# Decoder layer on one core: the cross-attention output turned and divided on VectorE in 32 x 32 blocks

## The chip, the cores and the metric

One core of a Trainium2 chip runs the whole kernel. The metric is device time in microseconds; the kernel before takes 612.61 us, the median of three runs between 610.9 and 614.4.

## What is computed

The input is x, 16 batches of 256 tokens with 256 features in float32. Three sublayers follow each other, each with a residual and a layer norm behind it (post-norm): a linear attention with relu features, a cross attention to a context of 256 tokens, and a low-rank feed-forward. The change touches the end of the cross attention:

```python
q = (query @ Wq.T), k = (key @ Wk.T), v = (value @ Wv.T)   # 16 heads of 16 features
q, k = rope2d(fp16(q), qpos), rope2d(fp16(k), kpos)
attn = softmax(q @ k^T * 16 ** -0.5)
x = (attn @ v).transpose(0, 2, 1, 3).reshape(B, Nq, C)
return x @ Wo.T + bo
...
x = layernorm(x + xattn(x, ctx, ...))
x = layernorm(x + gelu(x @ U1 @ V1 + b1) @ U2 @ V2 + b2)
```

## The kernel before

Every engine has its instruction list written out by hand, and semaphores tie them together. The main loop is unrolled over steps b = -3 to 15, and in a step several batches are in flight: batch b has its softmax and weighted sums computed, b + 1 its row maxima (`scores1`, `row_max`), b + 2 its q projection, b + 3 its linear attention; p = b - 1 is the batch whose attention output is divided, turned and projected, and q = b - 2 the one that goes through the second norm and the first feed-forward product. A step has eight slots. Each slot starts on TensorE with `scores1(b + 1, slot)`, which waits until VectorE's `row_max` of the slot before has emptied the one buffer SA, and `scores2(b, ...)`, which waits until ScalarE's exponential has emptied SB. The rest of each slot on every engine is listed in `step` of that engine, in strict order. So one engine that is late in a slot holds the others at the next score product.

The attention output of a batch goes this way. `pv` (line 1219) writes the weighted sums feature-major into the two PSUM banks BK[0] (first half of the heads) and BK[1]: 32 partitions for a head, of which 16 are features, the 17th the sum of the weights (the ones in `v_aug`), and 4 groups of heads by 256 tokens. ScalarE copies each bank to SBUF in `ev_pv` (line 633), to `o_fm`. TensorE turns it to token-major in `o_t` (line 1236), eight 128 x 128 transposes into BK[1] and FR[1]. VectorE takes the reciprocals (line 939) and multiplies (line 942) into `lin_tm` in `att_norm`. TensorE turns the result back in `att_t` (line 1133, BK[1]), four transposes. ScalarE copies it twice in `ev_att`: the high half, rounded to the matrix format (line 655), and the value itself (line 656, `att_raw`). GpSimd subtracts for the low half in `att_lo` (line 479). TensorE multiplies high and low halves with Wo in `wo` (line 1051, BK), and VectorE adds the residual in `add2` (line 950), takes statistics (line 887), and GpSimd normalises (`norm2`, lines 500 and 504) and keeps a copy with a bias (`keep_x2`, line 511).

Other pieces of the order that matter below: on TensorE `p_ff` (line 1264) follows `wo`, and `v2`, the v projection, goes into BK[0] and so waits until the first half of the weighted sums has left it. On VectorE a step runs `add1`, `ev_shift`, `row_max` 0, `stats2(q)`, `row_max` 1, `stats1`, `row_max` 2, `att_norm`, `row_max` 3, `k_halves`, `ev_x1`, `vk`, `row_max` 4, `rope_q` (lines 842, 859, 861), `ev_p` (line 907), `row_max` 5, `add2`, `lin` (lines 828 to 834), `row_max` 6, `rope_q_sum`, `lint`, `row_max` 7, `shift`. On GpSimd it runs `norm2(q)`, `rstd1`, `split_x` (lines 441 and 443), `att_lo`, `rope_k` (lines 467, 469, 473), `keep_x2(q)`, `residual2` (line 494), `residual_bias` (line 456), `split_c` (lines 441 and 443). SyncE places the turned k by eight DMAs once `rope_k` is done. After the last step the first block of the feed-forward (lines 1370, 1380, gelu at line 750) is interleaved by hand with what is left of batches 14 and 15; a loop over seven more blocks follows.

Of the kernel before, what the change touches and what calls it, by code (L numbers as in the profile page):

```python
# [31 lines left out]
P = 128  # L32
# [40 lines left out]
def build(nc, a):  # L73
    ctx = ExitStack()
    with ctx:
# [9 lines left out]
        def parts(name, shape):  # L85
# [78 lines left out]
        o_fm = sb("o_fm", [P, H2 // HC, T])  # L164

        stage_v1 = o_fm[:].rearrange("p q t -> p (q t)")


        rden2 = sb("rden2", [P, TT, H2])
# [62 lines left out]
        s_ot_mm, s_att_mm, s_wo_mm, s_x2t_mm, s_p_mm = map(  # L232
            sem, ("s_ot_mm", "s_att_mm", "s_wo_mm", "s_x2t_mm", "s_p_mm"))
# [347 lines left out]
        def _(act):  # L581
# [48 lines left out]
            def ev_pv(b, half):  # L630

                act.wait_ge(s_pv_mm, NQ * b + NQ // 2 * (half + 1))
                act.activation(o_fm[:, 2 * half:2 * half + 2].rearrange("p q t -> p (q t)"), BK[half][:], ACT.Copy
                               ).then_inc((s_pvc_ev, s_pvd_ev)[half], 1)

# [46 lines left out]
            def step(b):  # L682
# [12 lines left out]
                if on(p):  # L695
                    ev_pv(p, 1)
# [26 lines left out]
                if on(b):  # L723
                    exp_chunk(b, 4)
                    ev_pv(b, 0)
# [19 lines left out]
            ev_pv(LAST, 1)  # L745
# [34 lines left out]
        def _(dve):  # L780
# [177 lines left out]
            def step(b):  # L958
# [13 lines left out]
                if on(n):  # L972
                    stats1(n)
# [22 lines left out]
                if on(n1):  # L996
                    row_max(n1, 5)
# [486 lines left out]
```

## Time and profile before

| | us |
|---|---|
| median of three runs | 612.61 (610.9 to 614.4) |
| the profiled execution, its own time | 611.63 |
| its span on the core | 609.8 |
| TensorE busy | 531.0 (87%) |
| VectorE busy | 401.0 (66%) |
| ScalarE busy | 344.7 (57%) |
| GpSimd busy | 281.4 (46%) |
| the chain that ended last | TensorE 57%, VectorE 15%, issue 14%, GpSimd 6%, ScalarE 5% |

Busy time is a sum over the whole span; the chain is the sequence of work that the end waited for, followed back from the last instruction. What counts below is the row of steps between 100 and 440 us, which all look the same, and the end of the steps between 440 and 525 us.

### The profile page before, as it was taken

How to read it: one execution, taken by the hardware profiler on the slowest of the kernel's cores; microseconds unless marked ns; L12 is line 12 of the kernel's file. 1: busy time of each engine (PE TensorE's matmuls, PEld its weight loads, DVE VectorE, ACT ScalarE, POOL GpSimd, SP SyncE). 2: the span in 40 equal slices, each digit the busy share in tenths (PEclk: the TensorE clock that was granted, in tenths of full speed). 3: DMA queues.
4: the chain of work that ended last, by engine and by line, in shares of the span. 5: the costliest groups of instructions: out<-in, count | busy, mean ns of one | idle time of the engine just before them, and what ended most of it. 6: DMA issues, size and time to landing. Idle time of an engine off the chain costs nothing.

```text
span 609.8 us, 11786 instructions
## 1 busy us (share of the span) xinstructions
PE 531.0 (87%) x4224; PEld 366.8 (60%) x4224; DVE 401.0 (66%) x906; ACT 344.7 (57%) x503; POOL 281.4 (46%) x321
## 2 busy tenths in 40 slices
PE   0763879999999999999999999999987777999993
PEld 0652656767676767767676767677654444555551
DVE  4431688786968787777869687877877532253534
ACT  4420236756665666657566656666565566546551
POOL 3608526255564556364554645562624222233324
PEclk9995999999999999999999999999979889999997
DMA  7750120120202020111202020201101002032322
GB/s 263 177 140 14 53 65 13 55 63 5 83 2 82 7 77 27 57 34 51 79 5 84 2 82 7 79 26 41 29 3 31 19 1 70 17 104 103 104 102 103
DMA packets 27209, 35.99 MB, mean 59 GB/s; under 512 B 5592, under 2 KB 13400, under 8 KB 27160
## 3 DMA queue, kind: packets, MB, share of 16 engines
q1 hardware_dynamic: 26440, 34.90, 18.4%
q8 instruction: 32, 0.52, 0.4%
q10 hardware_dynamic: 720, 0.43, 0.3%
q14 instruction: 17, 0.14, 0.1%
HBM read 23.51 MB, written 8.65 MB: 53 GB/s over the span
## 4 chain that ended last, share of the span: by engine, by line
PE 57%; DVE 15%; issue 14%; POOL 6%; ACT 5%; DMA 2%; SPq 1%; POOLq 0%; ACTq 0%
PE FR L1051 20%; PE BK L1219 7%; PE BK L1051 7%; DVE nmax L914 6%; PE SC L1177 5%; PE SC L1204 3%; PE FR L1133 3%; PE FR L1109 2%; PE FR L1264 2%; DVE lin_tm L834 2%; POOL rs L568 2%; PE BK L1236 2%; POOL c_fm L573 2%; DVE y L950 1%; DVE rden L830 1%
## 5 line engine op out<-in xcount | busy, mean ns | idle before, releaser
L914 DVE TENSOR_REDUCE nmax<-SC 128x4 f32<-128x1024 f32 x128 | 156.2, 1220 | 42.1 <-PE SC L1177 41.1
L680 ACT ACTIVATE probs<-SC 128x1024 f32<-128x1024 f32 x128 | 131.1, 1024 | 69.9 <-PE SC L1204 69.6
L1177 PE MATMUL SC<-k_blk,q_grp 48*128 48x512 f16 x256 | 51.0, 395 | 27.1 <-DVE nmax L914 18.0
L1219 PE MATMUL BK<-probs,v_aug 128*32 128x256 f32 x1024 | 69.9, 390 | 0.5 <-ACT probs L680 0.5
L479 POOL TENSOR_TENSOR att_fm_l<-att_raw,att_fm_h 128x512 fp32r<-128x512 f32 x16 | 20.5, 1283 | 76.5 <-ACT att_raw L656 76.5
L500 POOL TENSOR_TENSOR rs<-ve,minus_half 128x2 f32<-128x2 f32 x16 | 11.2, 701 | 94.6 <-DVE nm L956 94.6
L1204 PE MATMUL SC<-q_grp,k_blk 64*128 64x256 f16 x512 | 50.3, 275 | 3.4 <-ACT q_grp L638 1.6
L750 ACT ACTIVATE probs<-SC,b_ff 128x512 f32<-128x512 f32 x64 | 39.8, 687 | 22.5 <-PE SC L1370 21.7
L1177 PEld LDWEIGHTS SC<-k_blk,q_grp 48*128 48x128 f16 x256 | 12.4, 93 | 54.8 <-issue 22.6
L1051 PE MATMUL FR<-w_qkv_h,xs_fm_h 128*128 128x512 f32 x64 | 29.2, 456 | 16.6 <-POOL xs_fm_l L443 14.1
L1219 PEld LDWEIGHTS BK<-probs,v_aug 128*32 128x32 f32 x1024 | 26.8, 110 | 25.9 <-issue 14.2
L609 ACT ACTIVATE kv_tm<-FR 128x512 f32<-128x512 f32 x32 | 19.1, 598 | 35.4 <-PE FR L1051 35.1
L1204 PEld LDWEIGHTS SC<-q_grp,k_blk 64*128 64x128 f16 x512 | 25.0, 97 | 21.2 <-ACT probs L680 4.1
L1380 PE MATMUL FR<-probs,w_u 128*64 128x512 f32 x128 | 35.5, 614 | 0.3 <-DVE xs_fm_l L1027 0.2
L568 POOL TENSOR_TENSOR rs<-ve,minus_half 128x2 f32<-128x2 f32 x16 | 11.0, 689 | 46.9 <-DVE nm L1039 46.9
L494 POOL TENSOR_TENSOR x1b<-x_tm,b_o 128x512 f32<-128x512 f32 x16 | 20.8, 1300 | 22.9 <-DVE y L950 22.9
L486 POOL TENSOR_TENSOR rs<-ve,minus_half 128x2 f32<-128x2 f32 x16 | 11.2, 698 | 42.9 <-DVE nm L896 42.9
L1034 DVE TENSOR_TENSOR x_fm<-BK,x_tm 128x512 f32<-128x512 f32 x16 | 10.4, 687 | 28.0 <-PE BK L1391 27.9
L1051 PEld LDWEIGHTS FR<-w_qkv_h,xs_fm_h 128*128 128x128 f32 x64 | 12.5, 196 | 26.1 <-POOL xs_fm_l L443 14.0
L1370 PE MATMUL SC<-p_fm,w_v_h 128*128 (+1 forms) x64 | 28.0, 438 | 0.0
L1051 PE MATMUL FR<-w_qkv_h,xs_fm_l 128*128 128x512 f32 x64 | 26.2, 409 | 0.0
L1051 PE MATMUL FR<-w_qkv_l,xs_fm_h 128*128 128x512 f32 x64 | 26.2, 409 | 0.0
(170 smaller groups left out, 1542.8 us busy)
## 6 DMA issues: line engine op xcount, KB each, us to landing
x_fm<-in_x_fm SPq DMA_DIRECT2D x16, 256.0 KB, 3.0
c_fm<-in_c_fm SPq DMA_DIRECT2D x16, 256.0 KB, 3.6
x_tm<-in_x_tm SPq DMA_DIRECT2D x16, 256.0 KB, 2.9
x_kept<-x2b SPq DMA_DIRECT2D x16, 256.0 KB, 2.3
x_tm<-x_kept SPq DMA_DIRECT2D x16, 256.0 KB, 2.8
out<-c_fm SPq DMA_DIRECT2D x16, 256.0 KB, 2.0
k_blk<-k_rope SPq DMA_DIRECT2D x128, 16.0 KB, 1.8
q_grp<-q_grp SPq DMA_DIRECT2D x32, 32.0 KB, 1.9
```

The costliest lines, as they stand in the source:

```text
L479: pool.tensor_tensor(flat(att_fm[1][:]), flat(att_raw[:]), flat(att_fm[0][:]).bitcast(F32), ALU.subtract).then_inc(s_attt_ev, 1)
L494: pool.tensor_tensor(x1b[:, n % NB], x1_tm[:], b_o2[:].unsqueeze(1).broadcast_to([P, TT, C]), ALU.add).then_inc(s_x1b, 1)
L568: pool.tensor_tensor(rs3[:, h], ve3[:, h], minus_half[:], ALU.pow).then_inc(s_rs3, 1)
L680: act.activation(probs[:, j % 4], SB[:], ACT.Exp, scale=SCALE).then_inc(s_exp, 1)
L750: act.activation(gel[:, f % 4], SC[f % 4 // 2][:].rearrange("p h t -> p (h t)")[:, FB * (f % 2):FB * (f % 2) + FB], ACT.Gelu_apprx_tanh, b ...
L914: dve.tensor_reduce(nmax[:, t, :, 2 * q:2 * q + 2], SA[:].rearrange("p (s f) t -> p s f t", s=2), AX.X, ALU.max, negate=True).then_inc(s_m ...
L1051: mm = pe.matmul(out, lhs(i, c), rhs(j, c), start=(c + k == 0), stop=(c + k == CC + 1))
L1177: mm = pe.matmul(SA[:, 2 * s:2 * s + 2].rearrange("p h t -> p (h t)"), q_grp[n % NB][rows, q, t * P:(t + 1) * P], k_blk[n % NB][rows, q].r ...
L1204: mm = pe.matmul(SB[:, 2 * s + f], k_blk[b % NB][rows, q, f, t * P:(t + 1) * P], q_grp[b % NB][rows, q], start=True, stop=True)
L1219: mm = pe.matmul(BK[q // 2][HP * k:HP * (k + 1), (q % 2) * T:(q % 2 + 1) * T], v_aug[b % NB][:, t, HC * q + k], probs[:, j % 4, k], start= ...
L1370: mm = pe.matmul(out, w_v1[k][:, f * P:(f + 1) * P], p_fm[:, bass.ds(i * FB, FB)], start=(k == 0), stop=(k == 1))
L1380: pe.matmul(FR[0][R * k:R * k + R, :], w_u2[:, f + k], gel[:, (f + k) % 4], start=(f == 0), stop=(f == NF - 2)).then_inc(s_u2_mm, 1)
```

## The change

The twelve TensorE transposes of a step and ScalarE's copies of the weighted sums go. VectorE turns each bank of weighted sums straight from PSUM in 32 x 32 blocks (`turn_pv`) into `o_tok`, where a partition holds a token of a block and a free index the head's features and weight sum. It takes one reciprocal, multiplies in two instructions into `lin_tm`, and turns that again in 32 x 32 blocks into `att_raw` in SBUF. The features come out in another order, which the rows of Wo are given on the host. ScalarE makes the high half from `att_raw` alone. The calls move as shown: `turn_pv(p, 1)` stands behind `stats1` and ahead of `row_max` 2, `turn_pv(b, 0)` behind `row_max` 5, and `add2` ahead of `row_max` 5. After the last step the orders of VectorE, ScalarE and TensorE change too.

```diff
-            def ev_pv(b, half):
-                act.wait_ge(s_pv_mm, NQ * b + NQ // 2 * (half + 1))
-                act.activation(o_fm[:, 2 * half:2 * half + 2].rearrange("p q t -> p (q t)"), BK[half][:], ACT.Copy
-                               ).then_inc((s_pvc_ev, s_pvd_ev)[half], 1)
             def ev_att(p):
-                act.wait_ge(s_att_mm, p + 1)
-                act.activation(flat(att_fm[0][:]), BK[1][:], ACT.Copy).then_inc(s_att_hi, 1)
-                act.activation(flat(att_raw[:]), BK[1][:], ACT.Copy).then_inc(s_att_raw, 1)
+                act.wait_ge(s_att_raw, p + 1)
+                wait(act, s_wo_mm, p)
+                act.activation(flat(att_fm[0][:]), flat(att_raw[:]), ACT.Copy).then_inc(s_att_hi, 1)
...
+            act.wait_ge(s_pv_mm, NQ * B)
             gelu(0, 0)
             gelu(0, 1)
             ev_att(LAST)
-            gelu(0, 2)
-            gelu(0, 3)
+            for f in range(2, 6):
+                gelu(0, f)
             ev_x2t(LAST - 1)
-            gelu(0, 4)
+            gelu(0, 6)
             ev_p(LAST - 1)
-            for f in range(5, NF):
-                gelu(0, f)
+            gelu(0, 7)
...
+            def turn_pv(b, half):
+                dve.wait_ge(s_pv_mm, NQ * b + NQ // 2 * (half + 1))
+                dve.transpose(o_tok[:, 2 * half:2 * half + 2].rearrange("p q b r -> p (q b r)"), BK[half][:]
+                              ).then_inc((s_pvc_ev, s_pvd_ev)[half], 1)
             def att_norm(p):
-                o = [t[:].rearrange("p (h r) -> p h r", r=HP) for t in (FR[1], BK[1])]
-                for k, t in enumerate((1, 0)):
-                    dve.wait_ge(s_ot_mm, 2 * p + k + 1)
-                    dve.reciprocal(rden2[:, t], o[t][:, :, D2]).then_inc(s_rden2, 1)
-                for k, t in enumerate((1, 0)):
-                    dve.wait_ge(s_rden2, 2 * p + k + 1)
-                    dve.tensor_tensor(lin_tm[:, t].rearrange("p (h d) -> p h d", h=H2), o[t][:, :, 0:D2],
-                                      rden2[:, t].unsqueeze(2).broadcast_to([P, H2, D2]), ALU.mult
+                dve.wait_ge(s_pvc_ev, p + 1)
+                dve.wait_ge(s_pvd_ev, p + 1)
+                dve.reciprocal(rden2[:], o_tok[:, :, :, D2]).then_inc(s_rden2, 1)
+                dve.wait_ge(s_rden2, p + 1)
+                out = flat(lin_tm[:]).rearrange("p (q b u d) -> p q b u d", q=2, b=T // HP, u=2)
+                for half in range(2):
+                    part = slice(2 * half, 2 * half + 2)
+                    dve.tensor_tensor(out[:, :, :, half], o_tok[:, part, :, 0:D2],
+                                      rden2[:, part].unsqueeze(3).broadcast_to([P, 2, T // HP, D2]), ALU.mult
                                       ).then_inc(s_att_ev, 1)
+                dve.wait_ge(s_att_ev, 2 * p + 2)
+                wait(dve, s_attt_ev, p)
+                dve.transpose(flat(att_raw[:]), flat(lin_tm[:])).then_inc(s_att_raw, 1)
...
                 if on(n):
                     stats1(n)
+                if on(p):
+                    turn_pv(p, 1)
...
-                if on(n1):
-                    row_max(n1, 5)
                 if on(p):
                     add2(p)
+                if on(n1):
+                    row_max(n1, 5)
+                if on(b):
+                    turn_pv(b, 0)
                 if on(m):
                     lin(m)
...
+            turn_pv(LAST, 1)
+            att_norm(LAST)
             stats2(LAST - 1)
-            att_norm(LAST)
             add2(LAST)
...
-            def vk(m, p):
+            def vk(m):
                 pe.wait_ge(s_kv1_ev, 2 * m + 2)
-                if on(p):
-                    pe.wait_ge(s_att_ev, 2 * p + 2)
...
-                if on(p):
-                    o_t(p, 1)
-                    o_t(p, 0)
...
-                if on(p):
-                    att_t(p)
                 if on(m):
-                    vk(m, p)
+                    vk(m)
...
-            o_t(LAST, 1)
-            o_t(LAST, 0)
...
             h_ff(0, 0)
             h_ff(0, 1)
-            att_t(LAST)
             h_ff(0, 2)
             h_ff(0, 3)
             u2_ff(0, 0)
             h_ff(0, 4)
             h_ff(0, 5)
+            wo(LAST)
+            u2_ff(0, 2)
             x2_t(LAST - 1)
-            wo(LAST)
             p_ff(LAST - 1)
-            u2_ff(0, 2)
             h_ff(0, 6)
             h_ff(0, 7)
```

## Rows read from the trace of the kernel before

**Rows 1.** Busy time by stretch: stretch, its length, each engine's busy us, clock, DMA share, GB/s.
```profile
core 0: us, PE busy (x) PEld busy (x) DVE busy (x) ACT busy (x) POOL busy (x), PEclk, DMA share, GB/s
298.85:326.79 27.94, 27.13 (x244) 19.64 (x244) 22.37 (x49) 18.02 (x27) 15.12 (x17) 1.00 0.15 46
438.52:511.14 72.62, 55.69 (x516) 32.60 (x516) 42.02 (x88) 42.66 (x57) 23.48 (x27) 0.88 0.08 26
511.14:525.79 14.65, 13.30 (x65) 7.74 (x65) 3.50 (x12) 9.05 (x15) 3.08 (x4) 1.00 0.05 19
```

**Rows 2.** The chain of waits of one step: start us, us, what (x instructions).
```profile
309.68 0.59 PE BK L1236 x4
...
310.26 0.44 PE FR L1236 x4
...
314.24 0.44 PE BK L1133 x4
...
315.66 0.32 PE SC L1177 x2
...
319.77 0.88 PE FR L1264 x4
...
321.94 1.23 DVE nmax L914
...
323.20 0.69 DVE y L950
...
326.79 0.39 PE SC L1177 x2
```

**Rows 3.** VectorE's timeline, same step: start us, us, instruction, idle before and its releaser.
```profile
309.50 1.23 DVE L914 TENSOR_REDUCE nmax<-SC 128x4 f32<-128x1024 f32 x1 [0.66 <-PE SC L1177]
...
311.27 0.41 DVE L942 TENSOR_TENSOR lin_tm<-FR,rden 128x256 f32<-128x256 f32 x1
...
312.47 1.22 DVE L914 TENSOR_REDUCE nmax<-SC 128x4 f32<-128x1024 f32 x1 [0.79 <-PE SC L1177]
...
319.34 0.45 DVE L859 TENSOR_TENSOR q_cos<-q,cos_t 128x512 f16<-128x512 f16 x1
...
319.72 1.37 DVE L861 TENSOR_TENSOR q_sin<-rot,sin_t 128x512 f16<-128x512 f16 x1
```

**Rows 4.** GpSimd's timeline, same step.
```profile
310.56 1.30 POOL L443 TENSOR_TENSOR xs_fm_l<-x_fm,xs_fm_h 128x512 fp32r<-128x512 f32 x1
...
315.99 1.28 POOL L479 TENSOR_TENSOR att_fm_l<-att_raw,att_fm_h 128x512 fp32r<-128x512 f32 x1 [4.13 <-ACT att_raw L656]
...
319.66 1.15 POOL L473 TENSOR_TENSOR k_rope<-k_cos,k_sin 128x512 f16<-128x512 f16 x1
```

**Rows 5.** Single source lines: ns min/median/max, first and last start us, form.
```profile
L950 DVE TENSOR_TENSOR y<-BK,x1b x16: 676/692/692, 127.7 to 520.3; 128x512 f32<-128x512 f32 x16
...
L808 DVE TENSOR_TENSOR w_v_l<-probs,w_v_h x1: 1422/1422/1422, 15.1 to 15.1; 128x512 fp32r<-128x512 f32 x1
...
L808 DVE TENSOR_TENSOR w_k_l<-x2b,w_k_h x1: 679/679/679, 16.4 to 16.4; 128x512 fp32r<-128x512 f32 x1
...
L842 DVE STREAM_SHUFFLE k_rot<-k x16: 436/439/442, 24.1 to 454.1; 128x256 uint32<-128x256 uint32 x16
...
L861 DVE TENSOR_TENSOR q_sin<-rot,sin_t x16: 412/1372/1479, 43.9 to 459.2; 128x512 f16<-128x512 f16 x16
```

**Rows 6.** The chain of waits of the last step.
```profile
494.29 0.61 ACT o_fm L633
...
500.26 1.27 POOL att_fm_l L479
```

**Rows 7.** Timeline across the end of the last step, VectorE and GpSimd.
```profile
506.17 0.75 DVE L887 BATCH_NORM_STATS2 st<-y 128x6 f32<-128x256 f32 x2
...
507.60 0.70 POOL L500 TENSOR_TENSOR rs<-ve,minus_half 128x2 f32<-128x2 f32 x1 [4.83 <-DVE nm L956]
...
509.58 1.27 POOL L511 TENSOR_TENSOR x2b<-x_tm,b_ff 128x512 f32<-128x512 f32 x1
...
517.19 1.29 POOL L479 TENSOR_TENSOR att_fm_l<-att_raw,att_fm_h 128x512 fp32r<-128x512 f32 x1 [6.34 <-ACT att_raw L656]
```

More of the change, by code:

```diff
@@ L163, in build @@
         shift16 = sb("shift16", [P, TT, P], F16)
-        o_fm = sb("o_fm", [P, H2 // HC, T])
-        stage_v1 = o_fm[:].rearrange("p q t -> p (q t)")
-        rden2 = sb("rden2", [P, TT, H2])
+        o_tok = sb("o_tok", [P, H2 // HC, T // HP, HP])
+        stage_v1 = o_tok[:].rearrange("p q b r -> p (q b r)")
+        rden2 = sb("rden2", [P, H2 // HC, T // HP])
         att_fm = parts("att_fm", [P, CC, T])
@@ L231, in build @@
         s_s1_mm, s_shift_mm, s_s2_mm, s_pv_mm = map(sem, ("s_s1_mm", "s_shift_mm", "s_s2_mm", "s_pv_mm"))
-        s_ot_mm, s_att_mm, s_wo_mm, s_x2t_mm, s_p_mm = map(
-            sem, ("s_ot_mm", "s_att_mm", "s_wo_mm", "s_x2t_mm", "s_p_mm"))
+        s_wo_mm, s_x2t_mm, s_p_mm = map(sem, ("s_wo_mm", "s_x2t_mm", "s_p_mm"))
         s_h_mm, s_u2_mm, s_ff_mm = map(sem, ("s_h_mm", "s_u2_mm", "s_ff_mm"))
@@ L694, in step @@
                     exp_chunk(b, 0)
-                if on(p):
-                    ev_pv(p, 1)
                 if on(m):
@@ L724, in step @@
                     exp_chunk(b, 4)
-                    ev_pv(b, 0)
                 if on(b):
@@ L744, in _ @@
             exp_chunk(LAST, 7)
-            ev_pv(LAST, 1)
             act.sem_inc(s_gelu, 4)
@@ L994, in step @@
                     ev_p(q)
+                if on(p):
+                    add2(p)
                 if on(n1):
                     row_max(n1, 5)
-                if on(p):
-                    add2(p)
+                if on(b):
+                    turn_pv(b, 0)
                 if on(m):
@@ L1222, in pv @@
                 mm.then_inc(s_pv_mm, 1)
-            def o_t(p, t):
-                if t == 1:
-                    pe.wait_ge(s_pvc_ev, p + 1)
-                    pe.wait_ge(s_pvd_ev, p + 1)
-                elif on(p + 4):
-                    pe.wait_ge(s_kv1_ev, 2 * (p + 4) + 1)
-                elif p + 4 == B:
-                    pe.wait_ge(s_proj_ev, B)
-                else:
-                    pe.wait_ge(s_p_ev, p - 1)
-                for q in range(H2 // HC):
-                    mm = pe.transpose((FR[1], BK[1])[t][:, q * P:(q + 1) * P], o_fm[:, q, t * P:(t + 1) * P], ident[:])
-                mm.then_inc(s_ot_mm, 1)
-            def att_t(p):
-                pe.wait_ge(s_att_ev, 2 * p + 2)
-                turn(BK[1], lin_tm, s_att_mm)
             def wo(p):
@@ L1255, in x2_t @@
                     pe.wait_ge(s_vk_ev, q + 6)
-                if q == LAST:
-                    pe.wait_ge(s_p_ev, LAST)
+                elif q + 5 == B:
+                    pe.wait_ge(s_proj_ev, B)
+                else:
+                    pe.wait_ge(s_p_ev, q)
                 turn(FR[1], x2_tm, s_x2t_mm)
@@ L1293, in step @@
                     scores2(b, 1)
-                if on(p):
-                    o_t(p, 1)
-                    o_t(p, 0)
                 if on(kn):
@@ L1307, in step @@
                     x1_t(n, m, kn)
-                if on(p):
-                    att_t(p)
                 if on(m):
-                    vk(m, p)
+                    vk(m)
                 if on(n1):
@@ L1446 @@
     by_group = [D2 * h + d for h in HEADS for d in range(D2)]
+    by_turned = [D2 * HEADS[HC * (2 * half + q) + k] + d
+                 for q in range(2) for k in range(HC) for half in range(2) for d in range(D2)]
     inv_freq = np.float32(1.0) / np.float32(100.0) ** (np.arange(0, 8, 2, dtype=np.float32) / np.float32(8))
@@ L1457 @@
         "w_v2": chunks(get["L0_xattn_Wv"].T[:, by_group]).reshape(P, -1),
-        "w_o2": chunks(get["L0_xattn_Wo"].T[by_group]).reshape(P, -1),
+        "w_o2": chunks(get["L0_xattn_Wo"].T[by_turned]).reshape(P, -1),
         "w_u1": chunks(get["L0_ffn_U1"]),
```

## The prediction

> **What bounds the kernel now.** I read the busy time by stretch first. One batch step, from the last score product of a batch to that of the next, takes 27.94 us, and TensorE is busy for 27.13 us of it at full granted clock; VectorE is busy for 22.37, ScalarE 18.02, GpSimd 15.12 [rows 1]. Steps 1 to 12 are alike, so twelve steps are the body of the kernel, the last three steps take 72.62 us at a mean clock of 0.88, and the start of the feed-forward part, up to the last batch's x2 transpose, takes 14.65 us [rows 1]. TensorE looks like the only bound, but the chain of waits says otherwise. From 309.68 to 320.65 it runs through TensorE without a gap: the attention output's transposes (0.59 and 0.44), the transposes of the divided output (0.44), the projections, and `p_ff` at its end [rows 2]. From there to the next score product at 326.79 it runs through VectorE: `row_max` 5 at 321.94, `add2` at 323.20, the linear attention's division, `row_max` 6 [rows 2]. A step is therefore some 21.8 us of TensorE order and 6.1 us of VectorE order. The third view is VectorE's timeline: it idles 0.66 us ahead of `row_max` 2 and 0.79 ahead of `row_max` 3 [rows 3]. That is all the room that lies beside the TensorE part at this place.
>
> **What the change does to a step.** It removes twelve TensorE transposes: 0.59 + 0.44 + 0.44 = 1.47 us of the chain [rows 2]. It removes three ScalarE copies out of PSUM; the fourth, for the high half, now reads SBUF. ScalarE is not on the chain here, so I cost these at nothing; what covers them is its 9.9 us of idle time per step, and no cover is lost. It adds three block transposes of 128 x 512 words to VectorE and turns the two reciprocals of 16 into one of 32.
>
> The price of a turn is in no row. The nearest by size and source is the 512-word read of PSUM in `add2`, 0.692; the nearest by kind is the shuffle of 256 words, 0.439; a turn that took each word twice would cost what `row_max` costs for 1024 words, 1.23 [rows 2, 5]. The bounds are 0.44 and 1.23. I take 0.70, because read and written words are the same as in `add2`, and the shuffle shows that moving words between partitions adds nothing that is seen.
>
> The Trainium skill (VectorE: DVE Perf Modes, The three transpose paths) gives 311 ns for a 128 x 128 bf16 transpose on VectorE, made of 32 x 32 blocks. With one more element per cycle at its 0.96 GHz this makes 0.71 us for 512, an estimate; it says nothing of four-byte words.
>
> Turn of the second half (`turn_pv(p, 1)`): it stands ahead of `row_max` 2, where VectorE idles 0.66 [rows 3]. 0.70 fits but for some 0.05. Free.
>
> The division (`att_norm`): it now starts right after `row_max` 2, at 310.80, and no longer waits for TensorE. Its products read both inputs from SBUF. GpSimd runs the subtraction for the next batch from 310.56 to 311.86 [rows 4], and two-input products of that sort are seen to wait for GpSimd: the product that began at 319.72 with GpSimd's own at 319.66 lasted 1.37 us where the shortest of its 16 took 0.412, and at the start of the kernel one weight half took 1.422 where its equals take 0.679 [rows 3 to 5]. So: reciprocal 0.3 to 311.15, first product held to 311.86 and done 0.3 later, second 0.35, 312.5. The third turn brings it to 313.2, `row_max` 3 (1.23) to 314.4. TensorE, 1.47 earlier, wants the fourth score product at 315.66 - 1.47 = 314.19 [rows 2]. It waits 0.2. With the small costs of that wait the front part gains 1.25 us.
>
> This hold is the Trainium skill's (SBUF — State Buffer, Who interferes with whom): a VectorE instruction with two SBUF inputs contends with a GpSimd one that reads SBUF, and the later one blocks until the first has finished. It speaks against this change, whose products read PSUM before; the 1.422 beside 0.679 agrees.
>
> Turn of the first half (`turn_pv(b, 0)`): it stands between `row_max` 5 and `lin`, inside the stretch where VectorE is the chain. Nothing hides it: +0.70. `add2` only trades places with `row_max` 5, both inside the stretch; the fifth score product starts 0.7 later after its own row maximum, where TensorE has `lin` and then idles. `v2` now waits for this turn instead of ScalarE's copy; it has 1.45 us to run and is through before `lin`'s division ends, so `lin_t` behind it waits for VectorE as it does today. ScalarE's `ev_att` waits for the third turn; it is ready about 313.2, when ScalarE is with the x1 copy. GpSimd's low half then begins at some 314.6 in place of 315.99 [rows 4], and `wo`, wanted at about 317.1, doesn't wait. No DMA is moved; the placement of k follows the low half on GpSimd and comes earlier.
>
> Net per step: -1.25 + 0.70 and 0.05 of seams = -0.5 us. Twelve steps: -6.0. Step 0 has the first-half turn with nothing removed: +0.7.
>
> **The last three steps.** Transposes run at half the clock there, and the route itself is on the chain: in the last step from ScalarE's copy at 494.29 to the end of the low half at 501.53, 7.24 us [rows 6]. The new route is 0.7 turn, 1.1 division, 0.7 turn, 0.7 copy, 1.3 low half and 0.5 for the exponential that ScalarE has in front: 5.0, so -2.2. The step before gives 1.6 by the same sum and pays 0.8 back at `add2` and the first-half turn. In step 13 the low half stands ahead of the k rotation whose placement ends the wait for the last scores: -2.2. Together -5.0, an estimate good to 2.
>
> **The start of the feed-forward part.** Here an order changes that costs. VectorE takes `turn_pv`, `att_norm`, and only then the statistics of batch 14, which today are done at 506.17, under the exponentials [rows 7]. GpSimd's order is unchanged: normalise batch 14, add the bias (from 507.60 to 510.85), and only then the low half of batch 15, at 517.19 [rows 7]. From the end of the last weighted sums: turn and division 2.7, statistics 1.4, GpSimd 3.3, low half 1.3: `wo` starts at 8.8 where it starts at 7.4 today. Behind it come, in TensorE's new order, a down-projection (1.0), the x2 transpose of 14, `p_ff`, and ScalarE's `ev_p` now behind the seventh gelu; VectorE's statistics of batch 15 wait for that. My sum to the last x2 transpose is 19.7 against 14.65 [rows 1]: +5.0, again good to 2. TensorE stands behind it in order, so it is all on the path; the loop after it is not touched.
>
> **Sum.** -6.0 + 0.7 - 5.0 + 5.0 = -5.3 us on the profiled execution's 611.63, so 606.3. That execution lies 1.0 under the median of the three runs, well inside their spread; I keep its own time as the base. About 0.5%, 3 us, is what a measurement of this kernel can tell from no change.
>
> **Rivals.**
> 1. *GpSimd's hold reaches the rotation of q.* Today the sine product ends at 321.09, 0.4 ahead of its need [rows 3]. `p_ff` comes 1.25 earlier, GpSimd's rotation of k 1.4 earlier. Its last product then starts at 318.2, and VectorE's cosine product, at 319.34 now, at 318.15: a dead heat. If GpSimd wins, the cosine product is held by the rotation and the sine product by the bias addition after it, and `row_max` 5 starts 0.7 late. The step is +0.2: 611.6 + 2.4 + 0.7 = 614.7. For it: the 1.37 us median; against it: the gap between GpSimd's two products. Chance 0.22.
> 2. *A turn costs 1.23.* The slower end. Place: the first-half turn in VectorE's stretch (+0.53), the other two in front of `row_max` 2 and 3 (+0.7 after idle time and hold are used up). A step is +0.7: +8.4, +0.7 and some 1.2 at the end: 622. It decides from a turn of about 0.92 us, where the step's gain is gone. Against it: the shuffle's price. Chance 0.14.
> 3. *The hold does not bite in the division.* Then `row_max` 3 ends in time and the step gives 0.75: 603.3. Chance 0.12.
> 4. *TensorE's clock.* Its idle time between the fifth and sixth score products grows from 0.7 to about 2 us. In the last steps, where it waited longer, the mean clock is 0.88 [rows 1]. If the granted clock fell to 1.2 GHz once per step, some 1.4 us of products would take twice as long: over 620. In all twelve steps today it is 1.00. Chance 0.05.
> 5. *It doesn't do what it says:* the removed transposes are made good by another wait, the exponentials or `row_max`, and the step stays 27.94: about 612. Chance 0.04.
>
> The forecast keeps 0.43; its own range is 602 to 610, from the two ends' estimates.
>
> **The numbers.** The range is 600 to 619: it takes in rivals 1, 3 and 5 and part of 2, and leaves out about 0.2. Faster by over 0.5%: the forecast but for 0.05, and rival 3: 0.50. Within: that 0.05, rival 5, and 0.14 of rival 1: 0.23. Slower: rivals 2 and 4 and the rest of 1: 0.27.
>
> **What would show it.** A turn at 0.70 us; the step at 27.4; `row_max` 3 later by 0.5 or more than `row_max` 2's end plus 2.0, with the first product longer than the second; the sine product ending before `ev_p` can start; the wait ahead of the last score product of a batch grown to over 1 us; the low half of batch 15 later than today against the last weighted sums. A turn over 0.9, or a product in the rotation that lasts beyond GpSimd's bias addition, makes the forecast wrong.

## The result: slower, 629.59 us, and the profile after

The kernel after takes 629.59 us, the median of four runs between 627.16 and 633.02. The kernel before, on the same chip, takes 613.13. The ratio is 1.0276, with an interval of 1.0217 to 1.0336. The forecast was 606.3, and its range ended at 619.

The profiled execution took 633.02 us, with a span of 631.2 against 609.8. TensorE is busy for 523.5 us (before 531.0), VectorE for 452.3 (401.0), ScalarE for 320.3 (344.7), GpSimd for 280.8 (281.4). From the page of the kernel after, part 4, the shares of the chain that ended last:

```profile
PE 36%; DVE 33%; issue 20%; POOL 5%; ACT 3%; DMA 1%; POOLq 0%; SPq 0%; DVEq 0%
```

Before, TensorE had 57% of that chain and VectorE 15%. The work did leave TensorE, but the path went with it. The windows of the kernel after, cut as in [rows 1] (one step, the last three steps, the start of the feed-forward part, and then the loop):

```profile
core 0: us, PE busy (x) PEld busy (x) DVE busy (x) ACT busy (x) POOL busy (x), PEclk, DMA share, GB/s
308.12:336.99 28.87, 26.14 (x230) 18.41 (x232) 26.18 (x51) 16.48 (x24) 15.05 (x17) 1.00 0.14 45
451.63:524.09 72.46, 55.38 (x481) 29.62 (x482) 47.13 (x88) 38.24 (x48) 19.64 (x22) 0.79 0.08 25
524.09:546.38 22.29, 15.50 (x53) 8.10 (x53) 6.05 (x19) 8.10 (x13) 6.06 (x8) 0.85 0.03 12
546.38:631.20 84.82, 73.94 (x328) 41.88 (x328) 34.89 (x121) 40.81 (x67) 29.44 (x49) 0.96 0.27 96
```

A step went from 27.94 to 28.87, though TensorE is busy for 0.99 us less in it. VectorE went from 22.37 to 26.18. That is 3.81 more where the three turns are 2.12, so some 1.7 us of it is VectorE's other instructions taking longer and not VectorE doing more. The spans differ by 21.4 us (the profiled execution is 3.4 over its median), and it adds up like this: 4.3 up to the first full step, 8.8 in twelve steps, -0.2 in the last three steps, 7.6 at the start of the feed-forward part, 0.8 in the loop. Of the twelve steps nine are longer by 0.9, one by 0.4, the last by 0.2, and the first, 26.88 us in both kernels, by nothing.

VectorE's timeline of that step in the kernel after; its counterpart is [rows 3]:

```profile
318.49 0.71 DVE L926 STREAM_TRANSPOSE o_tok<-BK 128x512 f32<-128x512 f32 x1
...
320.38 0.34 DVE L933 RECIPROCAL rden<-o_tok 128x32 f32<-128x32 f32 x1
320.76 1.45 DVE L938 TENSOR_TENSOR lin_tm<-o_tok,rden 128x256 f32<-128x256 f32 x2
322.25 0.71 DVE L943 STREAM_TRANSPOSE att_raw<-lin_tm 128x512 f32<-128x512 f32 x1
...
328.56 1.21 DVE L848 TENSOR_TENSOR q_cos<-q,cos_t 128x512 f16<-128x512 f16 x1
329.70 1.49 DVE L850 TENSOR_TENSOR q_sin<-rot,sin_t 128x512 f16<-128x512 f16 x1
331.22 0.43 DVE L896 TENSOR_TENSOR p_fm<-FR,p_hi 64x256 fp32r<-64x256 f32 x1
...
333.42 0.70 DVE L926 STREAM_TRANSPOSE o_tok<-BK 128x512 f32<-128x512 f32 x1
...
336.85 1.45 DVE L856 TENSOR_TENSOR q_grp<-q_cos,q_sin 128x512 f16<-128x512 f16 x1
```

GpSimd's timeline of the same step, its counterpart is [rows 4]:

```profile
320.30 1.29 POOL L442 TENSOR_TENSOR xs_fm_l<-x_fm,xs_fm_h 128x512 fp32r<-128x512 f32 x1
...
328.34 1.16 POOL L472 TENSOR_TENSOR k_rope<-k_cos,k_sin 128x512 f16<-128x512 f16 x1
329.46 1.46 POOL L510 TENSOR_TENSOR x2b<-x_tm,b_ff 128x512 f32<-128x512 f32 x1
...
336.75 1.27 POOL L442 TENSOR_TENSOR cs_fm_l<-c_fm,cs_fm_h 128x512 fp32r<-128x512 f32 x1
```

Lay the two beside each other. The division's products (320.76) end at 322.21, 0.6 after GpSimd's subtraction (320.30 to 321.59). The cosine product (328.56) ends 0.27 after GpSimd's k_rope ends; the sine product begins 0.24 after GpSimd's bias addition and ends 0.27 after it. The sum of the two (336.85) begins 0.10 after another subtraction, ends 0.28 after it, and takes 1.45 us; the shortest of its 16 takes 0.402. In what follows, such a product is called held.

The whole trace of the kernel after has 54 VectorE products with two inputs in SBUF (a pair counted once) that start while a GpSimd instruction that reads SBUF runs; 53 of them end 0.27 us or more after it. The odd one, at 443.73, starts 0.02 us behind GpSimd's k_rope (443.71) and takes 0.41, and k_rope takes 1.43: at so small a distance the times don't tell who was first. In the kernel before, four products of 512 columns start under GpSimd's memsets, which read nothing, and take 0.68 each; their equal that starts under a subtraction takes 1.42 [rows 5].

The sum of the rotation was held before too, but for less, by the rounding that stands ahead of GpSimd's subtraction. VectorE and GpSimd in the kernel before:

```profile
326.64 0.78 DVE L867 TENSOR_TENSOR q_grp<-q_cos,q_sin 128x512 f16<-128x512 f16 x1
```
```profile
326.54 0.61 POOL L441 TENSOR_SCALAR cs_fm_h<-c_fm 128x512 fp32r<-128x512 f32 x1
```

Against the last score product S of a batch, GpSimd's rounding starts at S - 0.94 in the kernel after and its subtraction at S - 0.24, where it was S - 0.25 and S + 0.45 before; the sum starts at S - 0.14 in both. So it now meets the subtraction.

What the step's 0.93 us is made of, counted from S (298.85 before, 308.12 after; before in brackets): the first projection behind it starts at S + 1.98 (S + 1.61), because the sum of the rotation is held; TensorE is through with q at S + 19.45 (19.49); `ev_p` starts at S + 23.10 (22.64); the next S is at 28.87 (27.94). So +0.37, then -0.41 in the front part, then +0.50 through the rotation, and +0.47 in VectorE's stretch with the turn.

The chain of waits of the kernel after, from the division to the transposes of x2, shows why the front part gave so little (compare [rows 2], where the same place is TensorE without a gap):

```profile
320.76 0.04 DVE lin_tm L938
320.79 1.00 issue
321.80 0.42 DVE lin_tm L938
322.25 0.71 DVE att_raw L943
322.96 1.06 DVE nmax L903
324.01 0.42 DVE k_rot L831
324.44 0.57 DVE x_fm_l L890
325.01 0.37 DVE vk_sb L809
325.38 0.14 issue
325.52 0.63 PE FR L1135 x4
```

The "issue" of 1.00 inside the division is the hold. Behind the row maximum come the shuffle of k, the low half of x1 and the copy of v and k, and only then may TensorE go on with the transposes of x2, which stand ahead of q's projection in its order.

### The profile page after: what moved, and what is told of

Its sections match the earlier page's. It is cut to its first block, busy times and chain, and to the rows that moved or that the text cites. A ratio compares the mean times of both kernels' runs of the same rounds, so it can differ in the third digit from the quotient of the medians.

```text
span 631.2 us, 11408 instructions
## 1 busy us (share of the span) xinstructions
PE 523.5 (83%) x4032; PEld 351.5 (56%) x4032; DVE 452.3 (72%) x938; ACT 320.3 (51%) x455; POOL 280.8 (44%) x321
## 4 chain that ended last, share of the span: by engine, by line
PE 36%; DVE 33%; issue 20%; POOL 5%; ACT 3%; DMA 1%; POOLq 0%; SPq 0%; DVEq 0%
PE FR L1055 17%; DVE nmax L903 9%; PE BK L1055 6%; PE BK L1221 3%; PE SC L1179 3%; DVE q_grp L856 3%; PE FR L1135 2%; DVE q_sin L850 2%; DVE q_cos L848 2%; DVE lin_tm L823 2%; POOL rs L567 2%; POOL c_fm L572 2%; DVE lin_fm_l L862 2%; DVE o_tok L926 2%; PE SC L1206 2%
## 5 line engine op out<-in xcount | busy, mean ns | idle before, releaser
L1221 PE MATMUL BK<-probs,v_aug 128*32 128x256 f32 x1024 | 72.8, 404 | 0.5 <-ACT probs L673 0.5
L1206 PE MATMUL SC<-q_grp,k_blk 64*128 64x256 f16 x512 | 51.9, 282 | 4.7 <-ACT probs L673 2.7
L1358 PE MATMUL FR<-probs,w_u 128*64 128x512 f32 x128 | 36.8, 629 | 0.7 <-ACT probs L739 0.7
L1135 PE MATMUL FR<-ident,x_tm 128*128 128x128 f32 x128 | 21.8, 295 | 10.9 <-DVE vk_sb L809 5.9
L1135 PEld LDWEIGHTS FR<-ident,x_tm 128*128 128x128 f32 x128 | 14.3, 147 | 23.8 <-issue 17.3
L926 DVE STREAM_TRANSPOSE o_tok<-BK 128x512 f32<-128x512 f32 x32 | 22.6, 706 | 6.7 <-PE BK L1221 6.7
```

The source lines that it names most:

```text
L926: dve.transpose(o_tok[:, 2 * half:2 * half + 2].rearrange("p q b r -> p (q b r)"), BK[half][:]).then_inc((s_pvc_ev, s_pvd_ev)[half], 1)
L1135: mm = pe.transpose(dst[:, c * T + t * P:c * T + (t + 1) * P], src[:, t, c * P:(c + 1) * P], ident[:])
L1206: mm = pe.matmul(SB[:, 2 * s + f], k_blk[b % NB][rows, q, f, t * P:(t + 1) * P], q_grp[b % NB][rows, q], start=True, stop=True)
L1221: mm = pe.matmul(BK[q // 2][HP * k:HP * (k + 1), (q % 2) * T:(q % 2 + 1) * T], v_aug[b % NB][:, t, HC * q + k], probs[:, j % 4, k], start= ...
L1358: pe.matmul(FR[0][R * k:R * k + R, :], w_u2[:, f + k], gel[:, (f + k) % 4], start=(f == 0), stop=(f == NF - 2)).then_inc(s_u2_mm, 1)
```

## Experiments

**1 and 2. GpSimd narrowed, in the kernel after and in the kernel before.** The same edit in both (shown for the subtractions). It leaves out most of GpSimd's subtractions for the inputs, its rotation of k and its kept copy of x2: they run over 32 of 512 columns, and the rest keeps old values.

```diff
-                pool.tensor_tensor(lo, x, hi.bitcast(F32), ALU.subtract).then_inc(s_lo, 1)
+                w = 2 * T if m < 2 else 32
+                pool.tensor_tensor(lo[:, 0:w], x[:, 0:w], hi.bitcast(F32)[:, 0:w], ALU.subtract).then_inc(s_lo, 1)
```

> The changed kernel, with GpSimd's two-input products narrowed: the low halves of x and the context from batch 2 on to 32 of 512 columns, the rotation of k from batch 1 on to 32 of 512, and the kept copy of x2 from batch 2 on to 32 of 512; the rest of these values is stale. All waits, orders and VectorE instructions stay. Theory 1 (GpSimd holds VectorE's products that read two SBUF inputs: the division, the rotation of q and the sum of the rotation): the products fall back to 0.42 us, a step from 28.87 to about 27.8 us, the kernel to about 616 us. Rival (the three turns alone fill VectorE, and the holds lie in idle time): at most 0.3 us per step, so 626 us or more.

> The kernel before with the same narrowing of GpSimd's products, as the control. Theory 1: there the holds lie beside other waits (the sine product ends 0.4 us before its need, the sum of the rotation ends before TensorE wants the projection), so a step loses at most 0.1 us: 610 to 613 us. If the holds were a cost of this kernel too, it would fall as much as the changed one, to about 600 us, and they would not explain the difference.

Measured: after, narrowed, 609.29 (ratio to before 0.9915, 0.9883 to 0.9947); before, narrowed, 608.06 (0.9918, 0.9887 to 0.9949). The narrowing takes 20.3 us from the kernel after and 5.9 from the kernel before. The two are then 1.2 us apart, within their intervals, though not alike inside: the step falls from 28.86 to 27.70 in the one and stays at 27.94 in the other, while the start of the feed-forward part still takes 20.3 us in the one and 14.7 in the other. The products are free: cosine 0.412, sine 0.418, sum 0.424, a division product 0.422.

```profile
L859 DVE TENSOR_TENSOR q_grp<-q_cos,q_sin x16: 404/424/439, 45.9 to 456.7; 128x512 f16<-128x512 f16 x16
```

So what made the step slow needs GpSimd's instructions at that length. A caution: the narrowing also hands over GpSimd's own results earlier; what that alone is worth was not taken apart. In the kernel before, and in version 6 (experiment 12), the same narrowing moved no step.

**3. VectorE's copy of v and k ahead of its low half of x1.**

```diff
-                if on(n):
-                    ev_x1(n)
                 if on(m):
                     vk(m)
+                if on(n):
+                    ev_x1(n)
```

> The changed kernel with VectorE's masked copy of the linear attention's sums (vk) ahead of its low half of x1, everything else as it is. Theory: what TensorE's removed transposes gain in the front of a step is lost at the x2 transpose, which waits for that copy, and VectorE reaches the copy late, behind row_max 3, the shuffle and the low half of x1; the copy earlier gives 0.3 to 0.4 us per step, about 625 us. Rival: the next score product or the q projection is as late as that, then nothing changes (628 to 631 us).

Measured: 620.11 (1.0106, 1.0065 to 1.0147), the step 28.02, so -0.84 instead of some -0.4. By the medians of eight steps, q's cosine product can start 0.31 earlier (S + 20.12 for 20.43), and that decides the race in the rotation the other way. The line of q's cosine product, kernel after and then this one (ns min/median/max of 16):

```profile
L848 DVE TENSOR_TENSOR q_cos<-q,cos_t x16: 409/1212/1286, 43.4 to 471.6; 128x512 f16<-128x512 f16 x16
```
```profile
L848 DVE TENSOR_TENSOR q_cos<-q,cos_t x16: 408/412/1004, 43.8 to 462.2; 128x512 f16<-128x512 f16 x16
```

It now starts ahead of GpSimd's k_rope and runs through in 0.41, and `ev_p` starts at S + 22.26 for 23.07: 0.31 us from the earlier q and 0.50 from the race. One move of 0.3 us is paid twice and more. The sum of the rotation is still held (median 1.447).

**4 and 5. The end.** In 4 only the statistics of batch 14 go back ahead of the turn; in 5 the orders of TensorE and ScalarE at the end also go back to those before.

```diff
+            stats2(LAST - 1)
             turn_pv(LAST, 1)
             att_norm(LAST)
-            stats2(LAST - 1)
```

> The changed kernel with VectorE's statistics of batch 14 ahead of the turn and division of batch 15 after the last step, as in the kernel before. Theory: GpSimd then normalises and keeps batch 14 under the last exponentials and the low half of batch 15 begins some 3 us earlier; the stretch from the last weighted sums to the last x2 transpose shrinks from 22.3 us to about 19, the kernel to about 626 us. Rival: the down-projection and the gelu order in front of it decide, and nothing changes.

> The changed kernel with the whole end as in the kernel before: statistics of batch 14 first on VectorE, x2 transpose of 14 ahead of wo and the down-projection on TensorE, gelu 4 ahead and gelu 5 to 7 behind ev_p(14) on ScalarE. Theory: the 7.6 us by which the stretch from the last weighted sums to the last x2 transpose grew are these orders; it falls from 22.3 to about 14 us, the kernel to about 621 us, some 4 us below the kernel with the statistics alone moved. Rival: TensorE's clock, at half in parts of that stretch (mean 0.85 against 1.00), keeps it at 18 us or more; then about 625.

Measured: 625.77 (1.0196, 1.0168 to 1.0224) and 622.59 (1.0127, 1.0079 to 1.0176). From the end of the last weighted sums to the last x2 transpose it is 22.3 us in the kernel after, 16.5 in 4, 13.2 in 5, and 14.65 before [rows 1]. The new orders at the end cost 7.0 us by the medians and 9.1 in this stretch, and with the old ones the turns make this stretch 1.4 us shorter than the transposes did.

Not all of the 9.1 is order. Experiment 3 keeps the orders of the kernel after here, and its stretch takes 19.8 us. In both, `wo` starts 8.6 us after the last weighted sums; behind it the clock differs. A part of the stretch in the kernel after, and the whole of it in experiment 3:

```profile
531.32:537.40 6.08, 4.76 (x16) 2.93 (x16) 0.69 (x1) 0.00 (x0) 1.26 (x2) 0.51 0.11 43
```
```profile
513.14:532.96 19.82, 13.02 (x52) 6.61 (x53) 6.05 (x19) 8.10 (x13) 6.06 (x8) 1.00 0.04 14
```

The profiled execution of the kernel after had half the clock for some 6 us, and that is 2.5 of its 22.3. Experiments 4 and 5 had 1.00 in the whole stretch, so at the same clock the two parts of the order cost 3.3 us each, 6.6 together, which agrees with the 7.0 of the medians.

**6. All three orders.** 3 and 5 together, and `lint`, the low half of the linear attention's output, for which TensorE's first projection waits, ahead of the sum of the rotation:

```diff
+                if on(m):
+                    lint(m)
                 if on(n):
                     rope_q_sum(n)
-                if on(m):
-                    lint(m)
```

> The changed kernel with the end of the kernel before, vk ahead of the low half of x1, and on VectorE the low half of the linear attention (lint) ahead of the sum of q's rotation. Theory: that sum is held by GpSimd's split of the context (1.44 us where 0.42 is free), and the projection on TensorE waits for lint behind it, 0.37 us per step; lint first frees it. A step of 27.65 us instead of 28.02, the kernel about 607 us (620.1 - 8 for the end - 4.5). Rival: the projection waits for something else, a step stays at 28.0, about 612.

Measured: 605.44 (604.27 to 606.74), ratio 0.9869 (0.9823 to 0.9914): 1.3% faster than the kernel before and 3.8% faster than the kernel after. Its windows, same cuts:

```profile
298.85:326.46 27.61, 26.20 (x231) 18.42 (x232) 24.55 (x50) 16.36 (x24) 15.25 (x17) 1.00 0.16 47
436.90:505.64 68.74, 50.74 (x481) 26.98 (x482) 47.15 (x94) 38.09 (x48) 22.57 (x26) 0.88 0.08 26
505.64:518.75 13.11, 11.67 (x52) 6.42 (x53) 4.92 (x13) 7.99 (x13) 3.23 (x5) 1.00 0.05 21
```

VectorE's timeline of the step. The division and the sine product are still held, the cosine product is not, and the sum (327.25) starts so late in GpSimd's subtraction that it is held for some 0.1 us only.

```profile
311.05 1.45 DVE L939 TENSOR_TENSOR lin_tm<-o_tok,rden 128x256 f32<-128x256 f32 x2
...
318.56 0.41 DVE L849 TENSOR_TENSOR q_cos<-q,cos_t 128x512 f16<-128x512 f16 x1
318.89 1.37 DVE L851 TENSOR_TENSOR q_sin<-rot,sin_t 128x512 f16<-128x512 f16 x1
320.68 0.43 DVE L897 TENSOR_TENSOR p_fm<-FR,p_hi 64x256 fp32r<-64x256 f32 x1 [0.42 <-ACT p_fm L663]
...
327.25 0.52 DVE L857 TENSOR_TENSOR q_grp<-q_cos,q_sin 128x512 f16<-128x512 f16 x1
```

`ev_p` starts at S + 21.83, 0.81 earlier than before, and the stretch behind it is 0.48 longer: the step gains 0.33. The last three steps give 3.9 us. The forecast had 0.5 and 5.0 for these two. The 3.9 is not a firm figure: the kernel after and experiments 4 and 5 have the same lists up to here, and their last three steps take 72.4, 70.0 and 71.7 us, so single executions differ by over 2 us in this place.

**7. The subtraction moved away from the division.** From 6, GpSimd's split for the next batch goes behind q's sine product, ahead of `keep_x2`:

```diff
-                if on(m + 1):
+                if b < -1 and on(m + 1):
                     split_x(m + 1)
...
+                if b >= -1 and on(m + 1):
+                    pool.wait_ge(s_q_part, 2 * n + 2)
+                    split_x(m + 1)
                 if on(q):
                     keep_x2(q)
```

> The same as three_orders, and GpSimd's split of the next x moved from ahead of the low half of the attention output to behind VectorE's sine product (with a wait for it), the kept copy of x2 behind that. Theory: the division's first product is no longer held (1.04 to 0.42 us), row_max 3 ends 0.6 us earlier, and the sine product is held at most once; a step of 27.3 to 27.5 us, about 604 us. Rival: TensorE's own order already sets the front part, so the step stays as in three_orders; or the moved split holds the rotation's sum later in the step and costs 0.2.

Measured: 609.06 (0.9914, 0.9887 to 0.9941), 3.6 us more than 6; the step is 27.87. The two division products now take 0.76 together and nothing comes of it: in the chain of waits, the way from ScalarE's copy of k and v to the transposes ahead of q's projection takes 6.18 us (311.50 to 317.68) as in 6 (309.18 to 315.36), and VectorE waits for TensorE there. GpSimd is late at the end of the step instead, and from its timeline and VectorE's:

```profile
301.15 1.29 POOL L442 TENSOR_TENSOR cs_fm_l<-c_fm,cs_fm_h 128x512 fp32r<-128x512 f32 x1
```
```profile
301.69 1.03 DVE L860 TENSOR_TENSOR q_grp<-q_cos,q_sin 128x512 f16<-128x512 f16 x1
```

The hold has moved to the sum of the rotation. `row_max` 7, the shift and `add1` stand behind the sum, and TensorE's first product with the next x starts at S + 4.38 for 4.10: this is the whole loss of the step. The division's hold, then, was real and is covered in 6.

**8. `add2` ahead of the sixth row maximum, in the kernel before.** The part of the change that has nothing to do with turns.

```diff
-                if on(n1):
-                    row_max(n1, 5)
                 if on(p):
                     add2(p)
+                if on(n1):
+                    row_max(n1, 5)
```

> The kernel before with only add2 moved ahead of row_max 5 on VectorE, as the change does. Theory: both lie in the same stretch of VectorE's order, nothing changes: 611 to 615 us, a step of 27.94. Rival: the fifth score product, 0.7 us later, delays the exponentials and v2 behind it and is part of the loss: 616 us or more.

Measured: 613.81 (0.9997, 0.9972 to 1.0022), which is no change of the time that could be told; the step in the trace is 27.80, 0.14 shorter. The order of [rows 2] shows where it comes from: `add2` behind the row maximum starts 1.26 us after it did (321.94 to 323.20), whereas the sum of the rotation starts 1.13 after one (307.99 behind 306.86 in the kernel after).

This run also tells what of the 4.3 us ahead of the first full step is not the change's. Its list up to there has no turn, and yet the first division of the linear attention starts at 105.23, against 101.72 before and 106.02 after. In the window from 62 to 90 us the mean clock is 0.86 here and 0.85 in the kernel after, where it was 0.97 before. With 3.5 of the 4.3 us also there without turns, 0.8 is left for the change, and that is no measurement: experiments 4 and 5, with the list of the kernel after up to there, reach the first full step 1.1 us later than it does.

**9. The orders without the turns.** The kernel before with two of the three orders, `vk` and `lint` as in 3 and 6 (the end has its old order anyway).

> The kernel before, with two of the three orders that the version at 605.4 us uses: VectorE's copy of v and k ahead of its copy of x1, and the division's transpose ahead of the sum of the two rotation products of q. No block turns. This asks whether that version's gain belongs to the turns or to the orders alone. Theory (the turns took a wait away from TensorE's order, and the new orders only undo the holds that the change brought): in the kernel before, TensorE's order sets the front part and q's cosine product is not held, so the step stays at 27.9 within 0.15 and the time within 0.5% of the kernel before (611 to 617). Rival (the orders are worth as much without the change): the step falls to 27.5 and the time to 608 or less, and the turns themselves are worth nothing or cost.

Measured: 619.94 (1.0094, 1.0066 to 1.0122), and the step is 28.56. Both expectations fall: the orders alone are neither neutral nor a gain, they cost 0.62 us per step. Most of it is a hold. With `lint` first, the sum of the rotation comes 0.9 us later than before and meets GpSimd's subtraction instead of the rounding ahead of it. VectorE's timeline and GpSimd's:

```profile
305.63 1.23 DVE L867 TENSOR_TENSOR q_grp<-q_cos,q_sin 128x512 f16<-128x512 f16 x1
```
```profile
305.29 1.29 POOL L443 TENSOR_TENSOR cs_fm_l<-c_fm,cs_fm_h 128x512 fp32r<-128x512 f32 x1
```

`row_max` 7, the shift and `add1` stand behind it in the chain of waits, and TensorE's first product with the next x starts at S + 4.57 for 4.10 before: 0.47 of the 0.62. In 6 GpSimd's subtraction starts at S - 0.25 instead of S + 0.46, so the sum, at S + 0.8 in both, takes 0.51 there. The rest shows at `vk`:

```profile
322.19 0.46 DVE L820 TENSOR_TENSOR vk_sb<-FR,vk_mask 128x288 f32<-128x288 f32 x1 [1.63 <-PE FR L1109]
322.56 0.68 DVE L901 TENSOR_TENSOR x_fm_l<-FR,x_fm_h 128x512 fp32r<-128x512 f32 x1
```

With `vk` first, VectorE waits 1.63 us for the v-k product, which stands behind the transposes of the divided output on TensorE, and the low half of x1, which q needs, comes behind that wait. That wait is long and costs little: q's projection takes 1.54 us in the chain where it took 1.41, so some 0.13. In 6, `vk` starts with no idle time ahead of it.

In the same orders the turns are worth 28.56 - 27.61 = 0.95 us per step, and 14.5 us in all. But half of that is the hold which `lint` first brings to the kernel without turns. Against the kernel before in its own order the turns with their orders are worth 0.33 per step. Whether `vk` first alone, or another order, would help the kernel without turns was not run.

**10. The third order alone.** 6 without the `lint` edit.

> The kernel after with the end in the order of before and VectorE's copy of v and k ahead of its copy of x1, but the sum of q's rotation left where it is. Against the version with all three orders it prices the third one alone. Theory: the sum of q's rotation is still held for 1.45 us, the division's transpose and the first projection start some 0.37 us late in each of thirteen steps, so the step is 28.0 and the time about 605.4 + 4.8 to 5.5 = 610 to 611. Rival (with the second order in place the sum of q's rotation is no longer on the path): the step is 27.65 and the time within 1.5 us of 605.4.

Measured: 610.28 (0.9951, 0.9925 to 0.9977), the step 28.01, the sum of the rotation 1.443. So with the low half behind it the hold costs 0.40 us per step, 4.8 us in twelve, and that is the whole difference to 605.44.

**11. One more turn per step.** In 6, the turn of the first half made twice, the second behind the first:

```diff
+                if half == 0:
+                    wait(dve, s_turn0, b)
+                    dve.transpose(out, BK[half][:]).then_inc(s_turn0, 1)
+                    dve.wait_ge(s_turn0, b + 1)
                 dve.transpose(out, BK[half][:]).then_inc((s_pvc_ev, s_pvd_ev)[half], 1)
```

> The version with all three orders, with the turn of the first half of the heads made twice, one behind the other, in each of sixteen steps: one more turn in VectorE's stretch between q's rotation and the last score product. Theory (that stretch is the path, nothing hides a turn there): 0.71 us and a seam of about 0.05 per step, the step goes from 27.61 to 28.3 or 28.4, the time to 605.4 + 16 x 0.72 = 616 to 617.5. Rival (TensorE, or the order behind it, hides part of it, as the change's own stretch grew by 0.47 and not by 0.70): 0.45 per step, about 612.

Measured: 617.95 (1.0059, 1.0030 to 1.0087), the step 28.34: +0.73, the full price of a turn and of the wait that ties the second to the first. Without such a wait the next instruction starts 0.63 after the turn does (333.42 to 334.05 in the kernel after).

**12. GpSimd narrowed in version 6.** The edit of 1.

> The version with all three orders, with GpSimd's low halves, its rotation of k and its kept copy of x2 narrowed to 32 of 512 columns (the rest keeps old values), as in the two narrowed runs before. It asks what the change is worth when GpSimd holds nothing: compare with the kernel before narrowed alike, 608.06. Theory (without holds the removed transposes give the front part 1.25 us and the turn costs 0.7 at most): the step is 27.2 to 27.4 and the time 599 to 602. Rival (the other waits, for the v and k copy and for ScalarE, keep the front part where it is): the step stays at 27.6 and the time is 603 to 605.

Measured: 601.93 (0.9810, 0.9754 to 0.9866), and the step is 27.60, that of 6 within 0.01. In version 6, GpSimd's holds cost nothing in a step any more. The 3.5 us lie outside these steps, as the 5.9 of the kernel before did. Against the kernel before, narrowed alike, the turns with their orders are worth 6.1 us. The rival holds for the step: other waits set the front part. What they are shows in the chain of 6:

```profile
307.56 1.61 PE FR L1056 x6
309.18 0.02 issue
309.20 0.61 ACT kv_tm L608
309.80 0.14 issue
309.94 1.67 PE FR L1056 x12
```

TensorE waits 0.75 us for ScalarE's copy of k and v, where in the kernel before it turned the attention output (0.59 + 0.44, [rows 2]). So 0.75 of the 1.03 us of these two groups is taken back by that copy.

## Why the prediction was wrong

**What failed, in one sum.** The forecast step was 0.5 us shorter, the measured one 0.93 longer. The difference of 1.43 is, in us: +0.84, the front part gained 0.41 and not 1.25; +0.50, the rotation of q, rival 1; +0.37, the sum of the rotation, which the prediction has nowhere; -0.28, VectorE's stretch with the first-half turn grew by 0.47 and not by 0.75. Experiment 1 takes 1.16 off the step (28.86 to 27.70) by shortening GpSimd's instructions, more than the 0.93 that the change had added.

**The turn at 0.70.** Right: 706 ns in the median of 32 from PSUM, 711 of 16 within SBUF. The estimate from the Trainium skill (VectorE: DVE Perf Modes, The three transpose paths) was 0.71, and the trace agrees with it for four-byte words too. Rival 2, a turn of 1.23, falls.

**The second-half turn free, the division held.** Both right: the turn fits ahead of `row_max` 2, and the division took 1.83 with its reciprocal, where the sum had 1.7. Rival 3 falls. The rule of the Trainium skill (SBUF — State Buffer, Who interferes with whom) agrees with the traces: 53 of the 54 overlaps of the kernel after, and the products under the memset, which weren't held.

**"With the small costs of that wait the front part gains 1.25 us."** This is the first step that failed; it gained 0.41. I followed one consumer of the late `row_max` 3, the score product, and took the rest of that wait for small costs. But `k_halves`, `ev_x1` and `vk` stand in order behind it on VectorE, and TensorE's transposes of x2, ahead of q's projection, wait for `vk`. Experiment 3 shows that the order of these matters. Most of the rest was never to be had: in experiment 1, with nothing held, `wo` starts at S + 18.62 for 19.32 before, so the front part gains 0.70. The first two groups of transposes stood where TensorE now waits for ScalarE's copy of k and v. I had costed ScalarE at nothing, on a share of busy time. For a part of the gain this is rival 5: another wait makes the removed transposes good.

**The first-half turn, +0.70 and 0.05 of seams.** The stretch grew by 0.47. A turn with no wait of its own holds up the next instruction by 0.63, and the swap of `add2`, which I took for nothing, gives 0.14 back (experiment 8).

**Rival 1, the dead heat in the rotation.** It happened, with the cosine product at 1.21 and the sine product at 1.49. GpSimd won by 0.22 us. I gave it a chance of 0.22. The race was lost by the step above: GpSimd's last product came 0.6 earlier against S instead of 1.4, and the cosine product 0.06 instead of 1.2. In itself its price was near: 0.50 where I had 0.7.

**The sum of the rotation, in no part of the prediction.** It is the next VectorE product with two SBUF inputs, and no part of the race: experiments 3 and 10 win that race and still have the sum at 1.447 and 1.443. Held for 1.45, it has the low half of the linear attention's output queued behind it, and TensorE's projection waits for that. Experiment 10 prices this at 0.40 per step. The prediction doesn't ask what GpSimd does when it runs.

**The twelve steps, -6.0.** They are 8.8 longer: 15 of the 26.7 us by which the profiled execution (633.02) missed its forecast (606.3). I also took the twelve for alike. The first takes 26.88 before and after, and the last is only 0.2 longer.

**The last three steps, -5.0.** They gave 0.2. (My own terms add up to 5.2.) In version 6 they gave 3.9; in the kernel after the mean clock is also 0.79 there, against 0.88 before and 0.88 in version 6. How much of the loss is hold and how much is clock was not taken apart, and executions of one list differ by over 2 us here, so neither the 0.2 nor the 3.9 settles whether the estimate was fair.

**The feed-forward start, +5.0.** Right in sign, cause and size, at full clock. The low half of batch 15 starts 7.2 us after the last weighted sums (predicted 7.5, before 6.1), and the stretch takes 19.8 us in experiment 3, which has the same orders there (predicted 19.7). The profiled kernel after has 7.6 more than before and not 5.0, for its clock was 0.51 for 6 us behind `wo`.

```profile
531.32 1.26 POOL L478 TENSOR_TENSOR att_fm_l<-att_raw,att_fm_h 128x512 fp32r<-128x512 f32 x1
```
```profile
535.60 0.69 DVE L949 TENSOR_TENSOR y<-BK,x1b 128x512 f32<-128x512 f32 x1 [7.56 <-PE BK L1055]
542.37 0.43 DVE L896 TENSOR_TENSOR p_fm<-FR,p_hi 64x256 fp32r<-64x256 f32 x1 [6.08 <-ACT p_fm L663]
```

These are GpSimd's and VectorE's timelines of the kernel after. The projection of batch 14 comes 6.1 us after VectorE has nothing else to do (4.8 in experiment 3), and the statistics of batch 15 stand behind it.

**Step 0, +0.7.** The 0.8 that is left once the slow start of experiment 8 is taken off is near it by luck: executions differ by more. **Rival 4** didn't occur in the steps: the granted clock is 1.00 in a step of the kernel after and of version 6.

## What to carry to other kernels

When work moves from TensorE to VectorE and its operands from PSUM to SBUF, list every VectorE instruction of the step that has two SBUF inputs, with GpSimd's schedule beside it, since the move shifts all of them and not only the new ones. Behind each held one, walk down VectorE's queue to every consumer, not to the nearest. Then re-order by hand: two of the three orders cost 0.6 us per step without the turns and, with them, all three turned a loss of 2.8% into a gain of 1.3%. The cost without the turns was for the most part again such a product that met another of GpSimd's instructions, so an order is tuned to one set of start times and has to be tuned again with the change. And before a stretch of one profile is laid to an order, compare its clock with that of another run that has the same order there.

## What the runs showed that I had not expected

A hold depends on who starts first, so a shift of 0.3 us was worth 0.84 per step (experiment 3). The two sides of such a race: a product that starts 0.24 us after GpSimd's (329.70 behind 329.46) takes 1.49, and one that starts 0.07 before it (318.56, with k_rope at 318.63) takes 0.41. And GpSimd, too, gets longer in these races: its k_rope took 1.34 in version 6, with VectorE's cosine product under way at its start, against 1.16 in the kernel after, where it was first.

```profile
318.63 1.34 POOL L472 TENSOR_TENSOR k_rope<-k_cos,k_sin 128x512 f16<-128x512 f16 x1
```

The turn itself was never held: all 32 from PSUM lie within 699 and 717 ns, and one of them (333.42) ran under GpSimd's two-input additions at 332.51 and 333.73.
